# A longer landing time for raw down-weight pieces in the plan of a sandwich kernel, with newly set due steps

## The reference

```python
def attn(x, W_in, b_in, W_out, b_out, gamma, beta):       # hidden 1024
    u = einsum('bsd,hd->bsh', x, W_in) + b_in
    def step(state, u_t):
        s = tanh(u_t + state * gamma + beta)
        return (s, s)
    _, states = scan(step, zeros, u)                       # 1024 steps
    return einsum('bsh,dh->bsd', states, W_out) + b_out

def ffn(x, gate_w, up_w, down_w, gate_scale, up_scale, down_scale):   # inner 1536
    q = lambda x, w, scale: einsum('bsi,io->bso', x, w.astype(float8_e4m3fn).astype(x.dtype)) * scale
    return q(silu(q(x, gate_w, gate_scale)) * q(x, up_w, up_scale), down_w, down_scale)

x = x + layernorm(attn(layernorm(x), ...))
x = x + layernorm(ffn(layernorm(x), ...))
```

## Time and profile before

| | |
|---|---|
| median of 3 runs | 558.2 us (555.98 to 560.86) |
| profiled execution | 558.66 us |
| its span, first to last instruction | 556.8 us |
| mean granted TensorE clock | 0.993 |
| step 0 of the recurrence starts | 16.55 us |

### The profile page before, as it was taken

The page is one execution under the profiler, slowest core; times in us unless marked ns, Lnnn a source line. Parts: engine busy times, 40 slices in busy tenths (PEclk is TensorE's granted clock), DMA queues, the critical chain, the costliest instruction groups (busy, mean ns, idle before and its releaser), DMA issues.

```text
span 556.8 us, 11947 instructions
## 1 busy us (share of the span) xinstructions
PE 539.2 (97%) x2958; PEld 457.0 (82%) x2958; DVE 446.4 (80%) x2608; ACT 375.3 (67%) x2317; POOL 228.7 (41%) x372
## 2 busy tenths in 40 slices
PE   8998989989899999999999999999999999999995
PEld 5856769878689888889788988898888887899994
DVE  3699999978798998878897978878987888874414
ACT  3687687864578777877677768777676767762332
POOL 1221446474546533562319313642352322643532
PEclk9999989999999999999999999999999999999998
DMA  8789398972014200120003000210002000200011
GB/s 268 260 257 250 88 232 156 252 132 63 20 40 153 58 2 1 39 97 1 2 1 114 21 1 2 77 39 2 1 2 77 1 2 1 77 2 1 1 39 38
DMA packets 25333, 39.92 MB, mean 72 GB/s; under 512 B 3760, under 2 KB 8496, under 8 KB 25264
## 3 DMA queue, kind: packets, MB, share of 16 engines
q1 hardware_dynamic: 19904, 30.24, 16.6%
q0 software_dynamic: 4608, 8.39, 8.9%
q10 hardware_dynamic: 752, 0.54, 0.3%
HBM read 26.57 MB, written 4.20 MB: 55 GB/s over the span
## 4 chain that ended last, share of the span: by engine, by line
PE 69%; DVE 3%; ACT 1%; issue 0%; POOLq 0%; DVEq 0%; POOL 0%
PE gate_up L1131 26%; PE wide L1087 16%; PE wide L1161 13%; PE wide L1056 12%; PE wide L1107 1%; DVE recur L1231 1%; DVE recur_second L1231 1%; DVE fused L1364 0%; ACT pairs L1556 0%; ACT gated L1591 0%; DVE z L1377 0%; DVE stats_z L1245 0%; DVE x_lo L1346 0%; DVE x_res L1304 0%; DVE y L1281 0%
## 5 line engine op out<-in xcount | busy, mean ns | idle before, releaser
L1556 ACT ACTIVATE pairs<-recur 128x8 f32<-128x8 f32 x768 | 137.8, 179 | 90.1 <-DVE recur L1231 90.0
L1231 DVE TENSOR_TENSOR_SCAN recur<-recur,pairs 128x16 f32<-128x16 f32 x768 | 151.1, 197 | 48.1 <-ACT pairs L1556 45.6
L1556 ACT ACTIVATE pairs<-recur_second 128x8 f32<-128x8 f32 x768 | 137.3, 179 | 0.0
L1231 DVE TENSOR_TENSOR_SCAN recur_second<-recur_second,pairs 128x16 f32<-128x16 f32 x768 | 133.4, 174 | 0.0
L1754 POOL TENSOR_TENSOR fused_lo<-fused,fused_hi 128x256 fp32r<-128x256 f32 x95 | 70.8, 747 | 140.0 <-ACT fused_hi L1609 137.8
L1087 PE MATMUL wide<-w_out_sb,pairs 128*128 128x512 f32 (+1 forms) x272 | 113.0, 563 | 0.2 <-ACT pairs L1565 0.2
L1056 PE MATMUL wide<-x_norm_t,w_in_sb 128*128 128x256 f32 x448 | 101.9, 382 | 3.6 <-ACT x_norm_t L1507 3.6
L1056 PEld LDWEIGHTS wide<-x_norm_t,w_in_sb 128*128 128x128 f32 x448 | 84.8, 191 | 16.1 <-ACT x_norm_t L1507 4.3
L1087 PEld LDWEIGHTS wide<-w_out_sb,pairs 128*128 128x128 f32 x272 | 75.4, 298 | 25.0 <-ACT pairs L1565 0.7
L1161 PE MATMUL wide<-down_q,fused_hi 128*128 128x512 f32 x192 | 80.3, 418 | 1.6 <-POOL fused_lo L1754 1.6
L1591 ACT ACTIVATE gated<-gate_up,gate_scale_cols 128x128 f32<-128x128 f32 (+1 forms) x169 | 63.6, 379 | 26.7 <-PE gate_up L1131 26.4
(11 more groups left out here) (135 smaller groups left out, 777.9 us busy)
## 6 DMA issues: line engine op xcount, KB each, us to landing
x_res<-x SPq DMA_DIRECT2D x16, 256.0 KB, 3.3
x_in<-x SPq DMA_DIRECT2D x14, 256.0 KB, 4.6
out<-z SPq DMA_DIRECT2D x14, 256.0 KB, 2.5
x_norm_t<-x_t SPq DMA_DIRECT2D x5, 512.0 KB, 4.4
raw_own<-rounders POOLq DMA_DIRECT2D x9, 256.0 KB, 5.2
w_in_sb<-w_in_t SPq DMA_DIRECT2D x4, 512.0 KB, 7.0
w_out_sb<-w_out_t SPq DMA_DIRECT2D x8, 256.0 KB, 5.2
raw_own<-down_w SPq DMA_DIRECT2D x8, 256.0 KB, 4.7
```

Of the source, the lines that this page charges most:

```text
L1231: eng.tensor_tensor_scan(preact_of[b].rearrange("p c k -> p (c k)"), factors_of[b].rearrange("p c k -> p (c k)"), pairs[:, t % RING, colum ...
L1556: ins = eng.activation(pairs[:, t % RING + 1, columns, 0], preact_of[b][:, :, 1], ACT.Tanh)
```

## The change

The plan gets a constant of its own, 15 steps, for the landing of the raw down pieces (24 to 35); pieces 0 to 23 keep 7. The five lists of due steps have new numbers, all of them; of these the diff shows two. No instruction is added or removed on any engine.

```diff
-ISSUE_STEPS, LOAD_STEPS, LOAD_LANDS = 1.0, 1.5, 7.0
+ISSUE_STEPS, LOAD_STEPS, LOAD_LANDS, SHARED_LOAD_LANDS = 1.0, 1.5, 7.0, 15.0
...
-CHUNKS_FROM = [36.9, 268.9, 388.4, 510.8, 673.4, 840.2, 1054.2, 1034.2]
+CHUNKS_FROM = [-157.3, 296.7, 394.8, 624.5, 536.4, 822.3, 1136.0, 1168.7]
...
-INPUTS_FROM = [-1344.6, 58.5, 202.4, 260.9, 828.6, 579.7, 684.4, 999.7]
+INPUTS_FROM = [-1494.9, -232.5, 349.4, 378.1, 904.9, 525.4, 785.3, 1102.9]
...
-    def load(name, after, parts=1):
+    def load(name, after, parts=1, lands=LOAD_LANDS):
 
         t.add("sync", name, ISSUE_STEPS * parts, after, 0.0)
         t.add("dma", ("landed", *name), LOAD_STEPS * parts, [(name, 0.0)], 0.0)
-        return [(("landed", *name), LOAD_LANDS)]
+        return [(("landed", *name), lands)]
...
-            landed = load(("raw", i), after)
+            landed = load(("raw", i), after, lands=LOAD_LANDS if i < GATE_UP_PIECES else SHARED_LOAD_LANDS)
```

More of the change, by code:

```diff
@@ L146 @@
 DOWN_RANK, NEGATE_RANK, ISSUE_RANK, PEAK_RANK, FIRST_X1_RANK, FIRST_CHUNKS_RANK = 20.0, 0.0, -2.0, 150.0, -4.0, -3.0
-CHUNKS_FROM = [36.9, 268.9, 388.4, 510.8, 673.4, 840.2, 1054.2, 1034.2]
-CHUNKS_PER_BLOCK = [9.5, 13.5, 7.5, 5.5, 9.5, 7.5, 2.5, 7.5]
-INPUTS_FROM = [-1344.6, 58.5, 202.4, 260.9, 828.6, 579.7, 684.4, 999.7]
-ROWS_FROM = [63.7, 150.2, 105.8, 112.0, 335.2, 313.5, 548.2, 566.0, 566.8, 537.6, 813.5, 752.1, 805.6, 836.1, 1124.2, 933.4]
-ROWS_TURNED = [177.8, 96.6, 277.1, 157.6, 351.1, 503.1, 395.2, 481.6, 757.2, 721.7, 947.8, 826.2, 1022.5, 863.0, 1070.9, 1030.1]
+CHUNKS_FROM = [-157.3, 296.7, 394.8, 624.5, 536.4, 822.3, 1136.0, 1168.7]
+CHUNKS_PER_BLOCK = [24.0, 36.5, 10.0, 13.0, 9.5, 5.0, 4.0, 5.0]
+INPUTS_FROM = [-1494.9, -232.5, 349.4, 378.1, 904.9, 525.4, 785.3, 1102.9]
+ROWS_FROM = [-162.4, -51.3, 25.1, 71.6, 446.8, 261.4, 562.8, 524.6, 635.2, 555.1, 891.5, 666.4, 940.4, 825.7, 1353.6, 1035.4]
+ROWS_TURNED = [153.5, -120.9, 373.0, 71.3, 302.5, 634.4, 377.3, 538.4, 822.7, 651.1, 978.3, 816.6, 935.2, 817.5, 1099.6, 1039.1]
 TENSOR_MARGIN = 1.0
```

## The result

| | before | after |
|---|---|---|
| median | 556.9 us (22 runs, 555.29 to 560.86) | 559.5 us (22 runs, 558.48 to 562.32) |
| ratio | | 1.0047 [1.0034, 1.0061] |
| profiled execution, span | 558.66, 556.8 us | 559.42, 557.6 us |

The change makes the kernel slower by 0.47%, 2.6 us. I had forecast 557.4 us against a median of 558.2: a small gain. With more runs the median of before is 556.9 us, and the execution whose trace I had read lies 1.7 us above that.

A forecast was written before the change was run, and what follows sets the result against it. Bound: TensorE's work plus gaps ended by the recurrence. Gains 2.06 + 0.80 - 0.50 = 2.4 us by step 256, plus 0.8 makes 3.2 at step 960, less 2.1 at the end: 1.1 gained, 557.4 us; eight in ten 554.0 to 561.5.

The forecast's parts named there:

- The stall that the new constant aims at: Last raw-piece conversions between VectorE's scans: waiting and long durations lose 2.06 us, all taken as gained (bounds 0.81 and 2.06).
- The first y: TensorE's wait for x_norm_t before u(2) lowers its clock, y(0, 1) comes late, a scan is held up: 0.80 us gained.
- What the change adds: Later conversions make settles later, so VectorE's peaks of down pieces wait: 0.5 us lost in all (bounds 0 and 3.3).
- The later blocks: Four scans held up by y copies waiting for TensorE, 1.7 us in sum; about half goes, 0.8 us gained.
- The last two blocks: y(7, 0) now ahead of its chunks waits for its state; the end gets 2.1 us further from step 960.
- Everything is gained: New peaks don't wait and all four y copies come in time: gain of 2.5 us, 556.0 us; chance 0.22.
- The slower case: Settles land late and VectorE stands at a peak with scans behind it: 560.4 to 563.7 us; chance 0.18.
- The wait only moves: Pieces land under the same load, VectorE waits as long at the new place: 2.06 us stay, 559.7 us; chance 0.10.
- the collision comes back: Conversions at the new place collide with GpSimd on the shared port pair: forecast plus 1.25, 558.7 us; chance 0.08.

The follow-up runs named there:

- The last experiment: Kernel before with both transposes of x(2) each put ahead of a round and their four copies ahead of four takes on ScalarE: 556.1 us, ratio 0.9984.
- after up to step 600: Two plans in one kernel: after's plan up to step 600, before's plan from there: 559.0 us, ratio 1.0027 to before.
- the first splice: Two plans in one kernel: after's plan up to step 275, before's plan from there: 557.6 us, ratio 1.0013 to before.

## Why the prediction was wrong, step by step

**The stall that the new constant aims at** is the step that failed first. I took 2.06 us of one execution as the price of an order. It is in one of six traces with that order; on average it is worth 0.3 us. (The kernel with the transposes of x(2) early keeps the order there and hasn't it either.) What I had in hand said so, and I passed over it: three times of before spread over 4.9 us, and 34 of 36 conversions ran undisturbed. A wait for a DMA that took 8.0 us where its neighbours took less needed more than one trace.

**The first y.** The chain was right: wait for x_norm_t, clock at 0.57, y late, scan held up. Eight traces have a wait of 2.06 to 2.24 us there. In six the granted clock fell to its lower level behind it, and VectorE then stood at the copy of y(0, 1); in two the clock stayed up, and it did not. The last experiment takes the wait away, and both are gone. The new order does this too: all traces with after's early order have a granted clock of 1.00 there. In the six traces of before's early order the clock of that window reads 0.57, 1.00, 0.59, 0.69, 0.71 and 0.62, and the hold-up at step 137 is 0.80, 0, 0.86, 0.60, 0.60 and 0.59 us. The last three lose another 0.5 at step 131, where the scan waits for its tanh. From step 120 to 150 the six take 15.6 us on average, and the one with the clock up 14.6: the chain is worth 1.0 us, a little more than the 0.80 that I took. (A slip without effect: the 0.23 us of the earlier trace rows is TensorE's idle time ahead of y(1, 1), not its distance from the last state.)

**What the change adds** is the term that was mis-sized most. I priced waits of peaks behind settles at 0.5 us. They went the other way: before's order has one, at step 221, worth 0.6 us on average, and after's has none. What does show is other work that moved too. In the trace of after, over the usual interval, the constant behind a late add takes 0.95 us, the two instructions that ran at half speed 0.36 and 0.66, and three intervals at steps 26, 74 and 127 another 0.19, 0.40 and 0.42: 3.0 us. All but the first come back in each of the five traces of after's order. The first is a chance of its own: 0.95, 0.33, 1.67, 0 and 0.55 us, 0.7 on average, so 2.8 us together. The mean times by stretch, in us:

| steps | before's order, six traces | after's order, five |
|---|---|---|
| 0 to 120 | 58.9 | 59.4 |
| 120 to 150 (clock, y(0, 1)) | 15.6 | 15.0 |
| 150 to 200 (late piece; constant) | 24.8 | 25.1 |
| 200 to 224 (peaks) | 12.3 | 11.7 |
| 224 to 256 | 16.0 | 16.8 |
| 0 to 256 | 127.5 (125.7 to 128.8) | 127.9 (127.3 to 128.9) |

The forecast for the last line was 2.4 us less; it is 0.4 more.

**The later blocks** were counted at 0.8 and look like nothing: from step 256 to 960 it is 322.6 us before and 322.4 after. Two opposite parts lie in that. From step 590 on the term came as forecast: VectorE's waits for copies of y fell from 1.8 us in all to 0.3, and the stretch takes 169.1 us, not 170.0. From step 256 to 590 after takes 153.3 us, not 152.6, partly by a new wait for a copy of y at 212 us (0.46 us, for TensorE).

**The last two blocks** were right, to the tenth: the end 2.1 us further from step 960 (88.8 or 88.9 in seven traces, 90.9 or 91.0 in six), TensorE waiting 1.38 us ahead of y(7, 0), inside the 1 to 3 that I gave. From y(7, 0) to y(7, 1) it is 30.6 us (forecast 30.7), from there to the end 60.2 (60.1). Of the 2.1 us, 1.0 is the down chunk that now stands behind the last y; most of the rest is that y(7, 1) starts 1.4 us behind the last state, not 0.6. By the earlier trace rows this loss could be read ahead of the run. Had I set the early terms to zero and left this one, the forecast would have been 2.1 us above before.

**Rivals.** "Everything is gained" fell with the early terms. The slower case had the right sign at 560.4 to 563.7 us, but not the mechanism: no peak waited. "The wait only moves" gave 559.7 us, 0.2 from the median, by luck: its 2.06 us to be kept were never a usual cost. It and "the collision comes back" each describe part of what is in after: a conversion waits at a new place, though for the add of its buffer's piece and not for its own, and two moved instructions took twice their time, the constant of piece 34 0.79 us and the x_norm 0.85. The page's rule on the shared port pair (the Trainium skill, "SBUF — State Buffer", section "SBUF: two separate sides") fits the traces in that both run beside a GpSimd subtraction that began first. Over all 16 traces 148 instructions of conversions and x_norms overlap such a subtraction. VectorE began first in 128, and 124 of these kept their time, 0.42 us at most; the other four are that of the earlier trace rows and three that began within 0.06 us of GpSimd's. GpSimd began first in 20: the ten with 0.48 us or more of it still ahead took 0.76 to 0.85 us, the other ten at most 0.55. No run here varies that subtraction alone, so the cause is argued from the order of starts, not shown. And the 1.25 us that the prediction puts on it are not borne out by the earlier trace rows, where the first long conversion began ahead of the subtraction, at 112.22 against 112.43 us.

The parts close: 0.4 us up to step 256, 0.7 to step 590, 0.85 back to step 960 and 2.1 at the end make 2.4 us (the last digits are of single traces), against 2.6 between the medians.

What stays open: what the wait at 171 us costs by itself. The two runs meant to show it didn't isolate it. What they give is a sum: from step 256 to 590 after up to step 600 has that wait and takes 0.6 us more than the first splice, which hasn't it, but other jobs of that stretch differ between the two as well. Open too is which job in block 7 makes the end longer; only the last blocks as a whole were tested.

## What to carry to other kernels

A stall that rests on one DMA's landing or on the clock's level in one trace may be a chance event, and then its worth is a price times a frequency: 2.06 us in one of six traces here, and for the constant of after anything from 0 to 1.67 us. A place in the order where TensorE must wait for a state came in every trace that had it. Weigh the second kind in full and the first by how often it shows, and take a second trace of the unchanged kernel before believing a gap of 2 us. In a planned order a change to one early cost reorders the last block as well, so read the order at the end first; two plans spliced at a seam tell the early part from the late one in a single run, if the seam moves no job that another engine waits for. A single job moved on one engine tells little, because the other engines keep the order that was woven around it.

## What the runs showed of the hardware

TensorE's clock was not the same function of the order in every execution. Behind the wait of about 2.1 us for x_norm_t, with the same instructions ahead of it, the granted clock from 78 to 82 us was 1.00 in one trace of before and 0.57 in the other; over all eight traces with that wait it was at 1.00 in two. Behind 2.87 us ahead of y(7, 0), and 1.93 us ahead of a down chunk at the same place, it read 0.57; behind 1.38 us ahead of y(7, 0) in after it read 1.00. Where the clock fell the hold-ups behind it cost about 1 us, so this is likely a part of why the runs of the kernel before spread over 5 us; the kernel whose edit takes the wait away spread over 2.8 us, before beside it over 3.5.
